# Attention block on one core: the transposes of the attention's output put directly behind the values of their slots, the output products spread differently

## The chip, the cores and the metric

The kernel runs on one core of one Trainium2 chip. The metric is the device time of one execution in microseconds (us), lower is better. A core has a matrix engine, TensorE (PE in the profile, its weight loads PEld), and three elementwise engines, VectorE (DVE), ScalarE (ACT) and GpSimd (POOL). SyncE (SP) issues the DMAs. Every engine runs its own program in order. They wait for each other by semaphores.

## What is computed

The input is 32 batches of 256 tokens by 128 channels. For each batch:

```python
xn  = layernorm(x)
a   = rmsnorm(xn);  q, k, v = a @ Wq, split(a @ Wkv)        # 16 heads of 64
q, k = head_rmsnorm(q), head_rmsnorm(k)
sim = tanh(q @ k.T / 50) * 50 / 8
att = (softmax(sim) @ v) @ Wo
h   = gelu(xn @ (W1 + scale * m1).T + b1)                  # m1, m2 of rank 4, from 16 rows of xn
out = x + att + h @ (W2 + scale * m2).T + b2
```

## The kernel before

The program is one pipeline over batches, fully unrolled. It goes in steps, one for each batch, and a step has eight slots, numbered 0 to 7 here. In slot s of step b the attention works on pair s of heads (two heads) of batch b. Beside that, the same slots hold pieces of other batches: projections of batch b+1 and b+2 (stage 1 and 2 in the tables), and the end of batch b-1 (stage -1): transposing its attention output, and multiplying it by Wo. Which piece stands in which slot of which engine is written out by hand in tables, TENSOR_STEPS, SCALAR_STEPS, VECTOR_STEPS and POOL_STEPS.

The pieces that matter here, with the line of the profile:

- `scores` (L531, TensorE): 12 matmuls for pair s. ScalarE then does `tanh` (L654, `clamped`) and `exp` (L661, `probs`), and GpSimd `lo` (L1073, `probs_lo`).
- `values` (L557 to L559, TensorE): 24 matmuls into the one bank `ps_o`, for the pair two slots back. VectorE then does `divide` (L844, L848, `o_sb`) and, for a pair four slots ahead, `normalise` (L826, `ps_n`), whose factors `rnorm` lie in the same bank as `ps_o`. So `values` of slot s waits for `normalise` of slot s-1: `wait(pe, qk_normed, min(PAIRS * n + s - 1 + NORMALISE_LEAD + 1, PAIRS * batches))`.
- `half` (L669, ScalarE) and `halves` (L835, VectorE): two half-precision parts of a normalised pair.
- `("q", k, a)`, `("k", k, a)`, `("v", k, a)`: projections, three matmuls each (L446 to L448). Piece k of four, called q0, q1 and so on below. ScalarE squares q pieces (L680) and VectorE scales them afterwards (L876); k pieces are copied by ScalarE (L686); v pieces by ScalarE (L691) and VectorE (L881).
- `("oT", k, -1)`: four transposes (L506) of `o_sb` for pairs 2k and 2k+1, copied by ScalarE into `oT` (L694). Called oT0 to oT3.
- `("xT", 0, 2)`, `("low", k, 0)` and `("hid", k, 0)`: transposes of the normed input, the low-rank part of the weights, and the hidden layer (L517), whose gelu is on ScalarE (L699, with an ACT_TABLE_LOAD ahead of it and another one ahead of the next `exp`).
- `("y", n)`: the next n of 24 output products (L567 for the hidden layer, L568 for `oT`) in `ps_y`. Product j of the first token tile needs, from j = 4 on, oT piece (j-4)/2.

All pieces with three entries write one of three banks of `ps_aux`, in turn, in the order of TENSOR_STEPS. Before TensorE writes one, it waits for the reader of the piece three before it (for a q piece that reader is L876 on VectorE, for k and oT pieces it is the copy on ScalarE):

```python
def wait_bank(eng, st, index):
    for back in range(1, 3 * len(AUX)):
        i = index - back * AUX_BANKS
...
        if STAGE[ahead] in (st.stages if rounds == 0 else st.before):
            s, per = AUX_READ[kind]
            wait(eng, s, per * PER_BATCH[kind] * st.batch(ahead + rounds)[0] + per * (k + 1))
            return
```

Of the kernel before, what the change touches and what calls it, by code (L numbers as in the profile page):

```python
# [48 lines left out]

AUX_BANKS = 3  # L50
TENSOR_STEPS = [
# [3 lines left out]
    [("scores",), ("values",), ("hid", 0, 0), ("hid", 1, 0), ("y", 3)],  # L55
# [4 lines left out]
]  # L60
AUX = [(s, *task) for s, tasks in enumerate(TENSOR_STEPS) for task in tasks if len(task) == 3]
assert len(AUX) % AUX_BANKS == 0
# [8 lines left out]


SCALAR_STEPS = [
    [("half", 3), ("q", 3, 1), ("tanh",), ("exp",), ("k", 2, 1), ("k", 3, 1)],
    [("half", 3), ("tanh",), ("oT", 0, -1), ("exp",), ("xT", 0, 2)],
    [("half", 3), ("tanh",), ("oT", 1, -1), ("exp",), ("oT", 2, -1)],
    [("tanh",), ("oT", 3, -1), ("exp",), ("hid", 0, 0), ("hid", 1, 0)],
    [("tanh",), ("q", 0, 2), ("exp",)],
    [("tanh",), ("q", 1, 2), ("exp",), ("v", 0, 1), ("v", 1, 1)],
    [("tanh",), ("exp",), ("k", 0, 2), ("k", 1, 2), ("v", 2, 1)],  # L80
    [("half", 3), ("tanh",), ("v", 3, 1), ("exp",), ("q", 2, 2)],
# [1059 lines left out]
```

How the kernel before makes its waits and increments, by code:

```python
        def wait(eng, s, value):  # L310
            if isinstance(value, int) and value <= 0:
                return
            eng.wait_ge(s, value)
# [38 lines left out]
        def wait_half_hi(eng, b, pair):  # L353
            if pair in GPSIMD_PAIRS:
                eng.wait_ge(half_hi_pool, len(GPSIMD_PAIRS) * b + GPSIMD_PAIRS.index(pair) + 1)
            else:
                eng.wait_ge(half_hi_made, len(SCALAR_PAIRS) * b + SCALAR_PAIRS.index(pair) + 1)
# [10 lines left out]
        @block.sync  # L369
# [19 lines left out]
            def load_rows(st):  # L389
                b, par, _ = st.batch(1)
                normed, used = [v if isinstance(v, int) else sp.to_reg(v) for v in (b + 1, 3 * b)]
                sp.wait_ge(xn_made, normed)
                if isinstance(b, int) and b == 0:
                    sp.wait_ge(rows_cleared, 1)
                wait(sp, sel_copied, used)
                for j in range(2):
                    for at in range(0, ROWS, BLOCK):
                        sp.dma_start(sel_raw[at:at + 2 * RANK, j], xn[1 + j:4 * RANK + j:2, par, 0])\
                            .then_inc(rows_loaded, 16)
# [1 line left out]
            def turn_heads(st, ahead, pair):  # L402
# [5 lines left out]
                        wait_half_hi(sp, b, pair)  # L408
                    else:
                        sp.wait_ge(half_lo_made, PAIRS * b + pair + 1)
                    sp.dma_start(heads_T[:, half, pair].rearrange("p t j n -> p (t j) n"),
# [26 lines left out]
            run_all(sp, run)  # L438
            for par in range(2):
                sp.wait_ge(y_stored[par], 16 * (batches // 2))
```

## Time and profile before

| | before |
|---|---|
| time, median of 3 runs | 1063.51 us (1062.15 to 1065.46) |
| the profiled execution's own time | 1067.33 us |
| its span, first to last instruction | 1065.1 us |
| TensorE busy (matmuls) / weight loads | 97% / 79% |
| VectorE / ScalarE / GpSimd busy | 88% / 92% / 92% |
| granted TensorE clock, mean | 0.994 |

Busy shares are averages over the span. Matmuls are pipelined, so a busy TensorE is not one at its peak; how much it waits is seen from the starts of its matmuls.

### The profile page before, as it was taken

What the parts mean: (1) busy time and instruction counts of PE and PEld (TensorE: products, weight loads), DVE (VectorE), ACT (ScalarE), POOL (GpSimd) and SP (SyncE); (2) the same over time, 40 slices, a digit from 0 to 9 for tenths busy, and PEclk for the clock granted to TensorE, in tenths of its full rate; (3) what the DMA queues carried; (4) which work ended last, traced back from release to release, by engine and by line L of the source; (5) the groups of instructions that cost most, each with busy time, mean ns of one, the idle gap of its engine ahead of it and who ended that gap; (6) DMA issues with size and microseconds to landing.
All of it is one profiled execution on the core that took longest, in us unless ns stands there. A gap on an engine that the chain in (4) does not pass through costs nothing.

```text
span 1065.1 us, 34270 instructions
## 1 busy us (share of the span) xinstructions
PE 1034.3 (97%) x12905; PEld 845.9 (79%) x12905; DVE 937.7 (88%) x2218; ACT 976.0 (92%) x1417; POOL 980.2 (92%) x912
## 2 busy tenths in 40 slices
PE   7689999999999999999999999999999999999997
PEld 6468888788888888888888888888888888888876
DVE  6998999988999988999998999998989998899972
ACT  4599999999999999999999999999999999999995
POOL 6799999999999999999999999999989999999883
PEclk8899999999999999999999999999999999999999
DMA  3354444444445435444444444444454444544351
GB/s 117 56 82 83 81 82 81 73 82 90 77 82 82 77 79 89 77 88 76 79 80 86 78 88 79 76 81 83 81 84 80 72 80 87 82 85 79 71 92 31
DMA packets 310491, 85.44 MB, mean 80 GB/s; under 512 B 282020, under 2 KB 309816, under 8 KB 310328
## 3 DMA queue, kind: packets, MB, share of 16 engines
q1 hardware_dynamic: 310328, 83.25, 43.6%
q8 instruction: 104, 1.70, 0.7%
q14 instruction: 59, 0.48, 0.2%
HBM read 11.09 MB, written 4.19 MB: 14 GB/s over the span
## 4 chain that ended last, share of the span: by engine, by line
PE 44%; POOL 26%; issue 10%; DVE 9%; ACT 5%; SPq 4%; DMA 2%; POOLq 0%; DVEq 0%; ACTq 0%
POOL probs_lo L1073 10%; PE ps_scores L531 9%; PE ps_y L568 5%; PE ps_aux L506 5%; POOL sq_k L1054 5%; POOL halves L1065 4%; PE ps_aux L517 4%; PE ps_o L557 4%; PE ps_aux L446 3%; PE ps_y L567 3%; PE ps_o L559 3%; PE ps_o L558 3%; POOL rstd L984 2%; DVE halves L835 2%; PE ps_aux L447 2%
## 5 line engine op out<-in xcount | busy, mean ns | idle before, releaser
L1073 POOL TENSOR_TENSOR probs_lo<-probs 128x1024 f16<-128x1024 f32 x256 | 485.1, 1895 | 20.6 <-ACT probs L661 19.5
L654 ACT ACTIVATE clamped<-ps_scores 128x1024 f32<-128x1024 f32 x256 | 265.4, 1037 | 43.4 <-PE ps_scores L531 36.3
L661 ACT ACTIVATE probs<-clamped 128x1024 f32<-128x1024 f32 x256 | 272.8, 1066 | 2.6
L557 PEld LDWEIGHTS ps_o<-v_hi,probs 128*128 128x128 bf16 x2048 | 183.7, 98 | 56.6 <-issue 53.5
L531 PE MATMUL ps_scores<-heads_T 64*128 64x256 f16 x3072 | 212.1, 271 | 5.0 <-ACT clamped L654 3.1
L557 PE MATMUL ps_o<-v_hi,probs 128*128 128x65 bf16 x2048 | 214.2, 195 | 2.7 <-DVE ps_n L826 1.1
L558 PE MATMUL ps_o<-v_lo,probs 128*128 128x64 bf16 x2048 | 211.8, 193 | 0.0
L559 PE MATMUL ps_o<-v_hi,probs_lo 128*128 128x65 bf16 x2048 | 211.3, 193 | 0.0
L446 PE MATMUL ps_aux<-w_hi,xhT_hi 128*128 128x512 f32 x384 | 175.3, 456 | 15.0 <-DVE qk L876 10.7
L558 PEld LDWEIGHTS ps_o<-v_lo,probs 128*128 128x128 bf16 x2048 | 187.5, 99 | 0.0
L559 PEld LDWEIGHTS ps_o<-v_hi,probs_lo 128*128 128x128 f16 x2048 | 187.4, 97 | 0.0
L826 DVE TENSOR_TENSOR ps_n<-qk,ps_o 128x512 f32<-128x512 f32 x256 | 175.8, 687 | 0.9 <-issue 0.6
L835 DVE TENSOR_TENSOR halves<-ps_n,halves 128x512 f16<-128x512 f32 x256 | 174.4, 681 | 2.4 <-ACT halves L669 1.4
L531 PEld LDWEIGHTS ps_scores<-heads_T 64*128 64x128 f16 x3072 | 129.3, 94 | 59.0 <-issue 22.8
L1065 POOL TENSOR_TENSOR halves<-qk,rnorm_sb 128x512 f16<-128x512 f32 x128 | 133.2, 1051 | 26.9 <-DVE rnorm_sb L815 14.4
L447 PE MATMUL ps_aux<-w_lo,xhT_hi 128*128 128x512 f32 x384 | 154.0, 401 | 0.0
L448 PE MATMUL ps_aux<-w_hi,xhT_lo 128*128 128x512 f32 x384 | 153.7, 400 | 0.0
L568 PEld LDWEIGHTS ps_y<-wo_sb,oT 128*128 128x128 f32 x1008 | 141.3, 191 | 11.5 <-ACT oT L694 0.9
L568 PE MATMUL ps_y<-wo_sb,oT 128*128 128x128 f32 x1008 | 148.6, 275 | 0.7 <-ACT oT L694 0.7
L1054 POOL TENSOR_TENSOR sq_k<-qk 128x512 f32<-128x512 f32 x128 | 130.7, 1042 | 5.2 <-ACT qk L686 2.9
L848 DVE TENSOR_TENSOR o_sb<-ps_o,rden 128x256 f32<-128x256 f32 x256 | 108.7, 425 | 8.8
L446 PEld LDWEIGHTS ps_aux<-w_hi,xhT_hi 128*128 128x128 f32 x384 | 73.9, 193 | 45.3 <-DVE qk L876 26.8
(96 smaller groups left out, 2009.7 us busy)
## 6 DMA issues: line engine op xcount, KB each, us to landing
heads_T<-halves SPq DMA_TRANSPOSE x512, 2.5
x_in<-in_L_attn_tokens_dram SPq DMA_DIRECT2D x32, 128.0 KB, 2.4
x_res<-in_L_attn_tokens_dram SPq DMA_DIRECT2D x32, 128.0 KB, 2.3
out_dram<-y_sb SPq DMA_DIRECT2D x32, 128.0 KB, 2.0
sel_raw<-xn SPq DMA_DIRECT2D x192, 4.0 KB
qk<-in_L_attn_Wkv_dram SPq DMA_DIRECT2D x2, 512.0 KB, 5.3
qk<-in_L_attn_Wq_dram SPq DMA_DIRECT2D x1, 512.0 KB, 3.5
qk<-in_L_ffn_W_dram SPq DMA_DIRECT2D x2, 256.0 KB
```

Of the source, the lines that this page charges most:

```text
L446: pe.matmul(o, hi_l, hi_r, start=True, stop=False)
L531: ins = pe.matmul(ps_scores[:, odd, t * seq:(t + 1) * seq], heads_T[rows, left, pair, t, k], heads_T[rows, right, pair, :, q], start=(i == ...
L557: pe.matmul(full, hi[:, col], v_hi[:, par, u, h], start=(u == 0), stop=False)
L558: pe.matmul(full[:, 0:DH], hi[:, col], v_lo[:, par, u, h], start=False, stop=False)
L559: ins = pe.matmul(full, probs_lo[:, buf, j, col], v_hi[:, par, u, h], start=False, stop=(u == TT - 1))
L568: return pe.matmul(o, oT[:, pair, tok], wo_sb[:, pair], start=False, stop=(pair == PAIRS - 1))
L654: nc.scalar.activation(clamped[:].rearrange("p j n -> p (j n)"), ps_scores[:].rearrange("p j n -> p (j n)"), ACT.Tanh).then_inc(clamp_done, 1)
L661: nc.scalar.activation(probs[:, pair % RING].rearrange("p j n -> p (j n)"), clamped[:].rearrange("p j n -> p (j n)"), ACT.Exp, bias=LIFT, ...
L835: v.tensor_tensor(halves16[:, pair % 4, 1].rearrange("p a n -> p (a n)"), ps_n[:], halves16[:, pair % 4, 0].rearrange("p a n -> p (a n)"), ...
L1054: g.tensor_tensor(sq_k[:, k % 2], part, part, ALU.mult).then_inc(k_squared, 1)
L1065: g.tensor_tensor(halves16[:, pair % 4, 0].rearrange("p a (h d) -> p a h d", d=DH), pair_of_qk(par, pair).rearrange("p a (h d) -> p a h d" ...
L1073: g.tensor_tensor(probs_lo[:, buf].rearrange("p j n -> p (j n)"), probs[:, buf].rearrange("p j n -> p (j n)"), probs[:, buf].rearrange("p ...
```

## The change

The oT transposes go from places late in slots 0, 1 and 2 (two in slot 2) to the place directly behind `values` in slots 0, 2, 3 and 4. The 24 output products of a step, before 0, 4, 4, 3, 4, 4, 2, 3 over the slots 0 to 7, are now 0, 4, 2, 2, 3, 4, 4, 5. ScalarE's table follows: oT0 ahead of k2 and k3, oT1 behind `exp` of slot 2, oT2 and oT3 between `tanh` and `exp` of slots 3 and 4, and q0 behind `exp` of slot 4 (before: ahead of it). VectorE's, GpSimd's and SyncE's order stay.

```diff
 TENSOR_STEPS = [
-    [("scores",), ("values",), ("k", 2, 1), ("k", 3, 1), ("oT", 0, -1)],
-    [("scores",), ("values",), ("xT", 0, 2), ("low", 0, 0), ("y", 2), ("oT", 1, -1), ("y", 2)],
-    [("scores",), ("values",), ("oT", 2, -1), ("low", 1, 0), ("y", 2), ("oT", 3, -1), ("y", 2)],
-    [("scores",), ("values",), ("hid", 0, 0), ("hid", 1, 0), ("y", 3)],
-    [("scores",), ("values",), ("q", 0, 2), ("q", 1, 2), ("y", 4)],
+    [("scores",), ("values",), ("oT", 0, -1), ("k", 2, 1), ("k", 3, 1)],
+    [("scores",), ("values",), ("xT", 0, 2), ("low", 0, 0), ("y", 4)],
+    [("scores",), ("values",), ("oT", 1, -1), ("low", 1, 0), ("y", 2)],
+    [("scores",), ("values",), ("oT", 2, -1), ("hid", 0, 0), ("hid", 1, 0), ("y", 2)],
+    [("scores",), ("values",), ("oT", 3, -1), ("q", 0, 2), ("q", 1, 2), ("y", 3)],
     [("scores",), ("values",), ("v", 0, 1), ("v", 1, 1), ("y", 4)],
-    [("scores",), ("values",), ("k", 0, 2), ("k", 1, 2), ("y", 2), ("v", 2, 1), ("v", 3, 1)],
-    [("scores",), ("values",), ("q", 2, 2), ("q", 3, 2), ("y", 3)],
+    [("scores",), ("values",), ("k", 0, 2), ("k", 1, 2), ("y", 4), ("v", 2, 1), ("v", 3, 1)],
+    [("scores",), ("values",), ("q", 2, 2), ("q", 3, 2), ("y", 5)],
 ]
 SCALAR_STEPS = [
-    [("half", 3), ("q", 3, 1), ("tanh",), ("exp",), ("k", 2, 1), ("k", 3, 1)],
-    [("half", 3), ("tanh",), ("oT", 0, -1), ("exp",), ("xT", 0, 2)],
-    [("half", 3), ("tanh",), ("oT", 1, -1), ("exp",), ("oT", 2, -1)],
-    [("tanh",), ("oT", 3, -1), ("exp",), ("hid", 0, 0), ("hid", 1, 0)],
-    [("tanh",), ("q", 0, 2), ("exp",)],
+    [("half", 3), ("q", 3, 1), ("tanh",), ("exp",), ("oT", 0, -1), ("k", 2, 1), ("k", 3, 1)],
+    [("half", 3), ("tanh",), ("exp",), ("xT", 0, 2)],
+    [("half", 3), ("tanh",), ("exp",), ("oT", 1, -1)],
+    [("tanh",), ("oT", 2, -1), ("exp",), ("hid", 0, 0), ("hid", 1, 0)],
+    [("tanh",), ("oT", 3, -1), ("exp",), ("q", 0, 2)],
```

On TensorE, in slot 2 of a step in the middle of the program, there stood behind the last matmul of `values` (the names in brackets are the semaphores that a row waits for):

```order
L506 MATMUL ps_aux<-ident,o_sb 128x128 [waits o_normed,xT_split]
L506 MATMUL ps_aux<-ident,o_sb 128x128 x3
L512 MATMUL ps_aux<-low2,sel_rows 128x512 [waits low_made,weff_made]
L568 MATMUL ps_y<-wo_sb,oT 128x128 [waits oT_copied]
L568 MATMUL ps_y<-wo_sb,oT 128x128
L506 MATMUL ps_aux<-ident,o_sb 128x128 [waits o_normed,oT_copied]
L506 MATMUL ps_aux<-ident,o_sb 128x128 x3
L568 MATMUL ps_y<-wo_sb,oT 128x128 [waits oT_copied]
L568 MATMUL ps_y<-wo_sb,oT 128x128
L531 MATMUL ps_scores<-heads_T 128x256 [waits clamp_done,heads_turned3]
L531 MATMUL ps_scores<-heads_T 128x256 x11
L557 MATMUL ps_o<-v_hi,probs 128x65 [waits qk_normed,o_normed,lo_made]
```

At the same place after the change:

```order
L506 MATMUL ps_aux<-ident,o_sb 128x128 [waits o_normed,k_copied]
L506 MATMUL ps_aux<-ident,o_sb 128x128 x3
L512 MATMUL ps_aux<-low2,sel_rows 128x512 [waits low_made,xT_split]
L568 MATMUL ps_y<-wo_sb,oT 128x128 [waits oT_copied]
L568 MATMUL ps_y<-wo_sb,oT 128x128
L531 MATMUL ps_scores<-heads_T 128x256 [waits clamp_done,heads_turned3]
L531 MATMUL ps_scores<-heads_T 128x256 x11
L557 MATMUL ps_o<-v_hi,probs 128x65 [waits qk_normed,o_normed,lo_made]
```

One group of transposes and two products have left the slot, so the scores and values of slot 3 (the last three rows) stand closer behind those of slot 2.

On ScalarE, slots 3 and 4 before the change, from `tanh` of slot 3 on to `tanh` of slot 5:

```order
L654 ACTIVATE clamped<-ps_scores 128x1024 [waits probs_done,scores_done]
L694 COPY oT<-ps_aux 128x512 [waits oT_filled]
L661 ACTIVATE probs<-clamped 128x1024 [waits attended,clamp_done]
L699 ACT_TABLE_LOAD
...
L654 ACTIVATE clamped<-ps_scores 128x1024 [waits probs_done,scores_done]
L680 ACTIVATE sq_q<-ps_aux 128x512 [waits norm2_made,q_filled]
L661 ACT_TABLE_LOAD [waits attended]
L661 ACTIVATE probs<-clamped 128x1024 [waits clamp_done]
L654 ACTIVATE clamped<-ps_scores 128x1024 [waits probs_done,scores_done]
```

And after it:

```order
L654 ACTIVATE clamped<-ps_scores 128x1024 [waits probs_done,scores_done]
L694 COPY oT<-ps_aux 128x512 [waits oT_filled]
L661 ACTIVATE probs<-clamped 128x1024 [waits attended,clamp_done]
L699 ACT_TABLE_LOAD
...
L654 ACTIVATE clamped<-ps_scores 128x1024 [waits probs_done,scores_done]
L694 COPY oT<-ps_aux 128x512 [waits oT_filled]
L661 ACT_TABLE_LOAD [waits attended]
L661 ACTIVATE probs<-clamped 128x1024 [waits clamp_done]
L680 ACTIVATE sq_q<-ps_aux 128x512 [waits norm2_made,q_filled]
L654 ACTIVATE clamped<-ps_scores 128x1024 [waits probs_done,scores_done]
```

The first L694 was oT3 and is now oT2, which TensorE makes in the same slot; the second is oT3; and L680, the square of q0, has moved behind the table load and `exp`.

On TensorE in slot 5, which is alike before and after but for the first wait, the two v projections now read:

```order
L446 MATMUL ps_aux<-w_hi,xhT_hi 128x512 [waits oT_copied]
L447 MATMUL ps_aux<-w_lo,xhT_hi 128x512
L448 MATMUL ps_aux<-w_hi,xhT_lo 128x512
L446 MATMUL ps_aux<-w_hi,xhT_hi 128x512 [waits q_scaled]
L447 MATMUL ps_aux<-w_lo,xhT_hi 128x512
L448 MATMUL ps_aux<-w_hi,xhT_lo 128x512
```

The second (v1) takes the bank of q0 and waits until VectorE has scaled q0, as it did before.

## Rows read from the trace of the kernel before

**Rows 1.** Busy time of each engine, stretches from 100 to 1000 us, summed

```profile
sum 900.00, PE 895.11 PEld 734.54 DVE 817.76 ACT 853.23 POOL 855.86; mean PE 99.46 PEld 81.62 DVE 90.86 ACT 94.80 POOL 95.10
```

**Rows 2.** Waits, 200 to 900 us (22 steps): total us, times, longest

```profile
PEld ps_aux L446 <- DVE qk L876: 12.2, 22, 1.0
```

**Rows 3.** Timeline, TensorE, one step: start us, length us, instruction, count

```profile
518.90 0.83 PE L531 MATMUL ps_scores<-heads_T 64*128 64x256 f16 x12
...
520.94 0.40 PE L448 MATMUL ps_aux<-w_hi,xhT_lo 128*128 128x512 f32 x1
521.41 0.50 PE L446 MATMUL ps_aux<-w_hi,xhT_hi 128*128 128x512 f32 x1
...
522.22 0.60 PE L506 MATMUL ps_aux<-ident,o_sb 128*128 128x128 f32 x4
522.75 0.83 PE L531 MATMUL ps_scores<-heads_T 64*128 64x256 f16 x12
...
528.99 0.60 PE L506 MATMUL ps_aux<-ident,o_sb 128*128 128x128 f32 x4
529.43 0.61 PE L568 MATMUL ps_y<-wo_sb,oT 128*128 128x128 f32 x4
529.97 0.83 PE L531 MATMUL ps_scores<-heads_T 64*128 64x256 f16 x12
...
530.73 0.20 PE L557 MATMUL ps_o<-v_hi,probs 128*128 128x65 bf16 x1
...
531.46 1.97 PE L517 MATMUL ps_aux<-xnT,w_eff 128*128 128x256 f32 x8
...
540.27 0.39 PE L446 MATMUL ps_aux<-w_hi,xhT_hi 128*128 128x512 f32 x1
...
540.96 0.38 PE L567 MATMUL ps_y<-w_eff,hid 128*128 128x128 f32 x2
...
550.68 0.83 PE L531 MATMUL ps_scores<-heads_T 64*128 64x256 f16 x12
```

**Rows 4.** Timeline, ScalarE, the same step

```profile
520.95 1.06 ACT L661 ACTIVATE probs<-clamped 128x1024 f32<-128x1024 f32 x1
521.91 1.09 ACT L686 COPY qk<-ps_aux 128x512 f32<-128x512 f32 x2
523.14 0.59 ACT L669 CAST halves<-ps_n 128x512 f16<-128x512 f32 x1
...
530.87 1.02 ACT L654 ACTIVATE clamped<-ps_scores 128x1024 f32<-128x1024 f32 x1 [0.68 <-PE ps_scores L531]
531.79 0.58 ACT L694 COPY oT<-ps_aux 128x512 f32<-128x512 f32 x1
532.25 1.07 ACT L661 ACTIVATE probs<-clamped 128x1024 f32<-128x1024 f32 x1
533.34 1.28 ACT L699 ACT_TABLE_LOAD   x1
534.63 1.57 ACT L699 ACTIVATE hid<-ps_aux,b_col 128x256 f32<-128x256 f32 x4
536.08 1.04 ACT L654 ACTIVATE clamped<-ps_scores 128x1024 f32<-128x1024 f32 x1
536.99 0.62 ACT L680 ACTIVATE sq_q<-ps_aux 128x512 f32<-128x512 f32 x1
537.62 1.28 ACT L661 ACT_TABLE_LOAD   x1
538.92 1.06 ACT L661 ACTIVATE probs<-clamped 128x1024 f32<-128x1024 f32 x1
```

**Rows 5.** Timeline, VectorE, the same step

```profile
523.94 0.68 DVE L835 TENSOR_TENSOR halves<-ps_n,halves 128x512 f16<-128x512 f32 x1
...
529.00 0.69 DVE L826 TENSOR_TENSOR ps_n<-qk,ps_o 128x512 f32<-128x512 f32 x1
...
538.80 0.66 DVE L876 TENSOR_TENSOR qk<-ps_aux,g_bc 128x512 f32<-128x512 f32 x1
```

## The prediction

> **What bounds the kernel now.** I first read the busy time over the steady part. TensorE's matmuls are busy 99.5% of it, GpSimd 95.1%, ScalarE 94.8%, VectorE 90.9% [rows 1]. With four engines so full, the shares don't say which one sets the pace. The starts in the timeline do. A step takes 31.78 us, from the scores of slot 0 at 518.90 to those of the next step at 550.68 [rows 3]. Inside it I looked for matmuls that start later than their like. There is one regular case: in slot 0, k3's first matmul starts 0.47 us behind the last one of k2 (520.94, 521.41), where such matmuls follow each other at 0.23 us. k3 then takes 0.81 us to the next group, where v1, with its bank free in time, takes 0.69 (540.27 to 540.96) [rows 3]. So this wait costs 0.24 + 0.1 us, about 0.34 in all. The list of waits has it as a weight load of L446 waiting for L876 on VectorE, once in each of 22 steps [rows 2]: k3's bank is that of q2, which VectorE has to scale first. Everything else on TensorE runs without a gap. TensorE is the bound, and it loses some 0.34 us of 31.78.
>
> The Trainium skill (Perfetto Trace Analysis, Identifying the Most-Contended Engine) says that matmul busy time is no measure for TensorE and that the share of weight loads is. That share is 81.6% here, under GpSimd's and ScalarE's. By that page TensorE has room, GpSimd would be the engine to watch, and a new order on TensorE should change little (the third rival below).
>
> **The work itself.** Nothing is added or removed: 16 transposes, 24 products and four copies a step, as before. What goes is a few changes between kinds of work. That is worth under 0.1 us a step in either direction, and I cost it at nothing. So the time comes from waits. I set t = 0 at the scores of slot 0 (518.90) and walk through a step of the new order. Four transposes take 0.44 us (528.99 to 529.43); two products take 0.54 (529.43 to 529.97), of which 0.09 is the change to scores, since four transposes ahead of scores take 0.53 (522.22 to 522.75) [rows 3]. So two products are worth 0.45.
>
> **Slot 0: the old wait goes.** k2 now needs q2's bank and k3 needs q3's. The transposes stand ahead of them, so k2 comes 0.44 later than before, but needs its bank about 0.7 earlier than k3 did. In itself that is 0.26 us worse. But more work (the sum of the last part below, 0.89 us) now lies between the reciprocal roots of slot 4, from which GpSimd's squares and VectorE's sums start, and this point. So I expect this wait to be gone: -0.34.
>
> **Slots 1 to 3: a new wait on VectorE.** Slot 1 loses a group of transposes (-0.44), slot 2 one group and two products (-0.89). The values of slot 3 stood at 530.73, t = 11.83 [rows 3]. TensorE now gets there at 11.83 - 0.34 - 0.44 - 0.89 = 10.16. They must wait for the `normalise` of slot 2. Before, it ran from 529.00 to 529.69, so it ended at t = 10.79 [rows 5], and slack was 1.04. Can VectorE be earlier? From the `halves` of slot 1 (523.94, t = 5.04) to that `normalise` it runs 12 instructions with no idle time [rows 5], and the change leaves their order alone. Their start hangs on ScalarE's `half` of slot 1. ScalarE's `exp` of slot 0 starts at 520.95 and the next instruction 0.96 later; a copy of oT takes 0.46 to the next (531.79 to 532.25), two k copies 0.98; `half` takes 0.59 [rows 4]. So with oT0 ahead of k2 the half ends at 2.05 + 0.96 + 0.46 + 0.98 + 0.59 = 5.04. VectorE's chain starts where it did, and ends at 10.79. TensorE waits from 10.16 to 10.84 (0.05 for the signal, as from a scaling to a matmul), and loses 0.07 to 0.1 on top, as k3 did: **about 0.75 us**. Queued behind it on TensorE are oT2, the hidden layer and all later slots.
>
> **Slots 3 and 4: ScalarE's chain.** Before, oT3 was long made when ScalarE came to it in slot 3. Now oT2 comes from the same slot. The values take 0.73 us (530.73 to 531.46) [rows 3]. The transposes take about 0.63 more until the last one ends, and ScalarE starts 0.07 behind such an end, as `tanh` does (scores end 530.80, `tanh` starts 530.87) [rows 3, 4]. So oT2's copy starts at 10.91 + 0.73 + 0.70 = 12.34. From there ScalarE has no gap [rows 4]: `exp` of slot 3 +0.46, table load +1.09, gelus +1.29, `tanh` of slot 4 +1.45, oT3 +0.91, table load +0.59, `exp` of slot 4 +1.30. That gives 19.43, where before it was 538.92, t = 20.02. And q0, which stood ahead of the table load at 536.99 (t = 18.09), now comes behind `exp`, +0.96: it starts at 20.39 and ends at 21.01.
>
> The table load is in this sum with 1.29 us, from its start to that of the first gelu (533.34 to 534.63) [rows 4]. The Trainium skill (ScalarE: Activation LUTs, What ACT_TABLE_LOAD costs) gives 2.66 us for a switch, a drain of 1.38 included. With that figure both loads would be longer, q0 would come 2.8 us later still, and the step would be some 36 us. The trace shows no such drain and decides.
>
> **Slot 5: v1 waits for q0.** v1 takes q0's bank, so it waits for q0's scaling on VectorE: 0.05 for the signal and 0.66 [rows 5], so at 21.72, and v1 starts at 21.77. Before, the scaling was done at 539.46, and v1 started at 540.27, t = 21.37, with 0.8 to spare [rows 3, 5]. Without waits TensorE would now be there at 21.37 - 0.34 - 0.44 - 0.89 + 0.22 + 0.22 = 20.14 (slots 3 and 4 each gain a group of transposes and lose a product); with the wait of slot 3, at 20.9. So it waits here again, **0.9 us**.
>
> **The step.** Behind v1 TensorE ran for 10.41 us to the next scores (540.27 to 550.68) [rows 3]. Slots 6 and 7 gain two products each, +0.89, and 0.1 is lost to the wait: 11.40. A new step is 21.77 + 11.40 = 33.17 us, 1.39 more than 31.78. It is a closed chain: scores of slot 0, ScalarE to `half` of slot 1, VectorE to `normalise` of slot 2, TensorE's values and oT2, ScalarE to q0, VectorE, v1, and TensorE to the next scores.
>
> The full pattern (q0 of the batch after next, v1 of the next, oT of the last) stands in steps 1 to 29. 29 x 1.39 = 40.3 us. Against the profiled execution's own 1067.33 that is 1107.6; it was 3.8 above the median of the runs, 1063.51, so for the median I get **1104**.
>
> **Rivals.** First, one of the two new waits does not bite, because I have placed VectorE's or ScalarE's chain too late. Without the wait at slot 3, the oT2 copy starts at 10.16 + 0.73 + 0.70 = 11.59, so everything behind it is 0.75 earlier: 32.42 us a step, +0.64 x 29 = +19, 1082. Against it: 12 instructions without idle time [rows 5]. 14%.
>
> Second, faster. If VectorE's `normalise` came by 10.1 and q0 were scaled by 20.1, only the removed wait would be left: -0.34 x 29 = -10, 1054. It turns on whether the last 1.6 us before q0's scaling can vanish; for it speaks only that ScalarE had idle time before (0.68 at one `tanh` [rows 4]), and I have already used that. 5%.
>
> Third, nothing: TensorE's order does not matter since GpSimd paces. GpSimd's 95.1% of 31.78 is 30.2 us of work [rows 1], so it could go on as before, and the time would stay within 0.3% (3.2 us, about what a measurement here can tell from no change). Against it: TensorE has no gaps but the one named. 5%.
>
> Fourth, more waits than I have seen. The scores of slot 3 are now 1.67 us earlier in the step, and the transposed heads that they need come by DMA, issued by SyncE at its own pace; or a wait that was hidden elsewhere comes out. 0.5 us more a step gives 33.7, +55, 1118. 14%.
>
> The forecast itself has 62%; its own range is 1093 to 1111, a third of a microsecond a step either way. The range 1081 to 1116 takes in the first rival and the nearer part of the fourth. Faster 0.05, same 0.05, slower 0.90.
>
> **What would show it.** In the profile after: no wait of L446 for L876 in slot 0, but one in slot 5, with v1's first matmul 0.9 us late. A wait of L557 for VectorE's `ps_n` (L826) once a step, in slot 3, about 0.7 us. ScalarE's q0 behind `exp`, and matmul busy time down from 99.5% to some 95 or 96%, GpSimd's and ScalarE's to about 91%. Slots 1 and 2 shorter, 6 and 7 longer by 0.45 each. I would be wrong if the `halves` of slot 1 started well before t = 5, or if v1's bank were free when TensorE comes.

## The result: 3.7% slower

The changed kernel takes 1103.72 us (median of 4 runs, 1102.64 to 1105.71), the kernel before 1064.49 us in the same comparison. The ratio is 1.0371, with a 95% interval of 1.0341 to 1.040. The profiled execution has a span of 1103.6 us where before it was 1065.1.

Over the same stretches as in [rows 1], the busy time of each engine is now:

```profile
sum 900.00, PE 856.84 PEld 703.13 DVE 780.14 ACT 823.79 POOL 824.24; mean PE 95.20 PEld 78.13 DVE 86.68 ACT 91.53 POOL 91.58
```

All engines have lost three to four points. They do the same work, in a longer step. The list of waits from 200 to 900 us (total us, times, longest) says where TensorE waits:

```profile
PEld ps_aux L446 <- DVE qk L876: 20.3, 21, 1.2
PE ps_aux L446 <- DVE qk L876: 11.1, 21, 0.7
PE ps_o L557 <- DVE ps_n L826: 10.5, 15, 0.7
PEld ps_scores L531 <- DMA heads_T<-halves: 8.3, 6, 1.7
PE ps_scores L531 <- DMA heads_T<-halves: 7.2, 6, 1.5
PE ps_o L557 <- DVE ps_o L803: 4.6, 16, 0.3
```

The first pair of rows is of the kind that stood in [rows 2], but it is another wait now, as the timeline shows. The third is new. The DMA wait is there in six of the 21 steps (the same list of the kernel before has it in one or two of 22). The last row is also new: the values waiting for the Newton steps (L801 to L807). With these, VectorE works out the reciprocal roots for `normalise`, in the bank of `ps_o`. TensorE in one step of the changed kernel, to be read beside [rows 3]:

```profile
540.03 0.83 PE L531 MATMUL ps_scores<-heads_T 64*128 64x256 f16 x12
...
542.46 0.39 PE L448 MATMUL ps_aux<-w_hi,xhT_lo 128*128 128x512 f32 x1
542.69 0.39 PE L446 MATMUL ps_aux<-w_hi,xhT_hi 128*128 128x512 f32 x1
...
549.38 0.83 PE L531 MATMUL ps_scores<-heads_T 64*128 64x256 f16 x12
...
550.91 0.19 PE L557 MATMUL ps_o<-v_hi,probs 128*128 128x65 bf16 x1 [0.70 <-DVE ps_n L826]
...
555.49 0.19 PE L557 MATMUL ps_o<-v_hi,probs 128*128 128x65 bf16 x1 [0.29 <-DVE ps_o L803]
...
560.89 0.40 PE L448 MATMUL ps_aux<-w_hi,xhT_lo 128*128 128x512 f32 x1
561.75 0.50 PE L446 MATMUL ps_aux<-w_hi,xhT_hi 128*128 128x512 f32 x1 [0.47 <-DVE qk L876]
...
573.07 0.83 PE L531 MATMUL ps_scores<-heads_T 64*128 64x256 f16 x12
```

The step takes 573.07 - 540.03 = 33.04 us. k3 in slot 0 follows k2 at 0.23 us (542.46, 542.69): the old wait is gone. In slot 3 the values wait 0.70 us for `normalise`. In slot 4 they wait 0.29 us for the Newton steps. In slot 5 v1 starts 0.86 us behind the matmul ahead of it, where 0.23 is usual: 0.63 us of wait. ScalarE and VectorE in the same step, beside [rows 4, 5]:

```profile
544.37 0.61 ACT L669 CAST halves<-ps_n 128x512 f16<-128x512 f32 x1
...
552.30 0.59 ACT L694 COPY oT<-ps_aux 128x512 f32<-128x512 f32 x1 [0.87 <-PE ps_aux L506]
552.78 1.06 ACT L661 ACTIVATE probs<-clamped 128x1024 f32<-128x1024 f32 x1
...
559.43 1.06 ACT L661 ACTIVATE probs<-clamped 128x1024 f32<-128x1024 f32 x1
560.40 0.58 ACT L680 ACTIVATE sq_q<-ps_aux 128x512 f32<-128x512 f32 x1
```

```profile
545.01 0.69 DVE L835 TENSOR_TENSOR halves<-ps_n,halves 128x512 f16<-128x512 f32 x1 [0.57 <-ACT halves L669]
...
550.08 0.68 DVE L826 TENSOR_TENSOR ps_n<-qk,ps_o 128x512 f32<-128x512 f32 x1
...
561.01 0.69 DVE L876 TENSOR_TENSOR qk<-ps_aux,g_bc 128x512 f32<-128x512 f32 x1 [1.46 <-ACT sq_q L680]
```

One sees the whole chain. ScalarE's half of slot 1 (t = 4.34 from the step's start) releases VectorE, which had idled 0.57 us for it. VectorE reaches `normalise` at t = 10.05. TensorE's values follow, then oT2, for which ScalarE had idled 0.87 us. ScalarE runs on without a gap to q0 (t = 20.37), for which VectorE had idled 1.46 us, and v1 waits for its scaling. Idle time with a releaser stands at each handover, none in between.

### The profile page after: what moved, and what is told of

It is laid out like the page before. It is cut to its first block, busy times and chain, and to the rows that moved or that the text cites. A ratio compares the mean times of both kernels' runs of the same rounds, so it can differ in the third digit from the quotient of the medians.

```text
span 1103.6 us, 34270 instructions
## 1 busy us (share of the span) xinstructions
PE 1030.4 (93%) x12905; PEld 842.3 (76%) x12905; DVE 931.4 (84%) x2218; ACT 981.9 (89%) x1417; POOL 980.9 (89%) x912
## 4 chain that ended last, share of the span: by engine, by line
PE 38%; ACT 27%; DVE 13%; issue 10%; SPq 6%; DMA 4%; POOL 1%; ACTq 0%; DVEq 0%; POOLq 0%
ACT probs L661 8%; PE ps_scores L531 7%; PE ps_aux L446 6%; PE ps_y L568 5%; PE ps_aux L448 4%; PE ps_aux L447 4%; ACT L699 4%; ACT L661 3%; ACT hid L699 3%; DVE halves L835 3%; ACT clamped L654 3%; DMA heads_T<-halves 3%; PE ps_o L557 3%; DVE ps_n L826 3%; PE ps_y L567 3%
## 5 line engine op out<-in xcount | busy, mean ns | idle before, releaser
L568 PE MATMUL ps_y<-wo_sb,oT 128*128 128x128 f32 x1008 | 144.4, 276 | 2.8 <-ACT oT L694 2.8
L876 DVE TENSOR_TENSOR qk<-ps_aux,g_bc 128x512 f32<-128x512 f32 x128 | 85.0, 685 | 47.2 <-ACT sq_q L680 47.2
```

What stands on the lines that cost most here:

```text
L568: return pe.matmul(o, oT[:, pair, tok], wo_sb[:, pair], start=False, stop=(pair == PAIRS - 1))
```

## The experiments

Theory 1 is the chain above: one closed chain through TensorE, ScalarE and VectorE, with another one close behind it, which runs through VectorE's Newton steps. Its rivals were that the waits are independent of each other, or that they are slack which something else would take. Step lengths below are medians over steps 1 to 29, from the starts of slot 0's scores. Places in a step (t) are from the same start, in steps of the usual length.

### q0 ahead of `exp` again

```diff
-    [("tanh",), ("oT", 3, -1), ("exp",), ("q", 0, 2)],
+    [("tanh",), ("oT", 3, -1), ("q", 0, 2), ("exp",)],
```

> The changed kernel with one edit: in slot 4 ScalarE does q0 ahead of exp again (tanh, oT3, q0, exp). Theory 1 (one closed chain, in which v1 waits for q0's scaling): q0 starts at t = 17.95 instead of 20.37, v1's bank is free when TensorE comes, its wait of 0.63 + 0.1 us a step goes, and the wait of slot 3's values for VectorE stays. A step of 33.05 becomes 32.3 us, 21 us less than the changed kernel: about 1083, ratio to the kernel before 1.018. Rival A (v1's wait is only where slack shows, and another wait takes its place, for instance that exp of slot 4, 0.45 us later, delays GpSimd and the values of slot 6): no gain, 1100 to 1104. Rival B (the two new waits are independent and this one is the whole of the loss beyond slot 3's 0.75 us): same as theory 1 in time, told apart by the third kernel of this batch.

Measured: 1083.67 us, ratio to the kernel before 1.019 (1.0172 to 1.0207), and a step of 32.31 us. Its waits from 200 to 900 us:

```profile
PE ps_o L557 <- DVE ps_n L826: 12.2, 18, 0.8
...
PE ps_o L557 <- DVE ps_o L803: 5.1, 18, 0.3
...
PEld ps_aux L446 <- DVE v_lo L881: 0.7, 3, 0.3
```

No wait for L876 is left, the others have about the size that they had, and 0.74 us a step is back. So in the changed kernel q0's place in ScalarE's table costs 20 us of the 39.

### One sum of squares behind slot 2's `normalise`

```diff
-    ... ("normalise",), ("sum", 5, 1), ("sum", 6, 1), ("xT", 0, 2), ("low", 0, 0)],
-    [("halves", 3), ("divide",), ("normalise",), ("sum", 7, 1), ("low", 1, 0)],
+    ... ("normalise",), ("sum", 5, 1), ("xT", 0, 2), ("low", 0, 0)],
+    [("halves", 3), ("divide",), ("normalise",), ("sum", 6, 1), ("sum", 7, 1), ("low", 1, 0)],
```

> The changed kernel with one edit: VectorE sums the squares of one k piece (0.6 us) behind the normalise of slot 2 instead of in slot 1. No work changes, only the normalise of slot 2 comes 0.6 us earlier. Theory 1: slot 3's values start at t = 10.2 instead of 10.8, oT2's copy, the table loads, exp and q0 follow 0.6 earlier, so v1 starts at about 21.1 instead of 21.7, and a step is 32.3 to 32.4 us: 20 us less, about 1084, ratio 1.018. TensorE then waits in slot 4 for the Newton steps instead (about 0.9 us, no work saved, since that chain on VectorE is as long as before). Rival (slot 3's wait for VectorE is slack that v1's wait would swallow anyway, and ScalarE's own queue sets q0): no change, 1100 to 1104.

Measured: 1097.3 us, ratio 1.031 (1.0286 to 1.0334), a step of 32.67 us. The step is 0.38 us shorter, half of what theory 1 said, and more than the rival's nothing. The time gained only 6.4 us of the expected 20. Part of that is in the longer steps: the profiled execution has nine that are over 0.25 us longer than its median, the changed kernel seven. VectorE's timeline in slot 1 shows why the step gained only half:

```profile
542.31 0.68 DVE L778 TENSOR_REDUCE norm<-sq_q 128x8 f32<-128x512 f32 x1
543.11 0.42 DVE L767 TENSOR_TENSOR xhT_lo<-ps_aux,xhT_hi 128x256 fp32r<-128x256 f32 x1
...
545.25 0.69 DVE L826 TENSOR_TENSOR ps_n<-qk,ps_o 128x512 f32<-128x512 f32 x1
```

L767 starts 0.80 us behind the sum, where 0.6 is usual: VectorE now comes to it before ScalarE has copied the transposed input. So slot 2's `normalise` comes only 0.4 us earlier, and the Newton steps 0.2 us later. A step that is 0.38 us shorter fits the 0.4. But this explanation came after the fact, so the next edit repeats the test without that side effect.

### The low-rank weights behind slot 2's `normalise`

```diff
-    ... ("normalise",), ("sum", 5, 1), ("sum", 6, 1), ("xT", 0, 2), ("low", 0, 0)],
-    [("halves", 3), ("divide",), ("normalise",), ("sum", 7, 1), ("low", 1, 0)],
+    ... ("normalise",), ("sum", 5, 1), ("sum", 6, 1), ("xT", 0, 2)],
+    [("halves", 3), ("divide",), ("normalise",), ("low", 0, 0), ("sum", 7, 1), ("low", 1, 0)],
```

> The changed kernel with one edit: VectorE makes the low-rank weights of the hidden layer (L888, 0.66 us) behind the normalise of slot 2 instead of ahead of it. It repeats the test of the moved sum without that one's side effect (there VectorE came 0.2 us too early for ScalarE's copy of the transposed input and waited, so normalise came only 0.4 us earlier, and the Newton steps 0.2 later). Theory 1: normalise 0.66 us earlier, Newton steps where they were in the changed kernel, q0 and v1 0.65 earlier: 32.3 to 32.4 us a step, about 1083, ratio 1.018. Rival (the chain does not run through slot 3's wait; what the moved sum gained had another cause): 32.7 or more, 1095 to 1104.

Measured: 1088.33 us, ratio 1.0219 (1.0203 to 1.0235), a step of 32.40 us. The step is as expected, 0.65 us shorter with no work removed: VectorE's order ahead of slot 2's `normalise` is on the chain. The time is 5 us above the forecast. In the profiled execution six steps are 0.7 to 1.6 us longer than the rest (in the changed kernel six steps, by 0.4 to 0.8); the list of waits has the DMA wait of the scores in four of those between 200 and 900 us, which is taken up below (the edit that removes it was not tried on this kernel). TensorE now waits in slot 4 instead:

```profile
PE ps_o L557 <- DVE ps_o L803: 16.3, 18, 0.9
```

### Both: q0 ahead, and the sum behind `normalise`

The edits are those of the first and second experiment together.

> The changed kernel with both edits above. Theory 1: they are not additive. VectorE's Newton steps end at t = 15.35 as before, the values of slot 4 wait for them, and from there TensorE needs 16.9 us to the next scores: 32.3 us a step again, 1083, ratio 1.018, like each edit alone. Rival B (two independent waits): both go, 31.6 us a step, about 1062, ratio 0.998.

Measured: 1087.14 us, ratio 1.0221 (1.0203 to 1.0238), a step of 32.53 us. Independent waits would have given 31.6 us. Instead the two edits together are no better than q0 alone (32.31), and 0.2 us worse, which is the 0.2 by which the moved sum delays the Newton steps. Its waits:

```profile
PE ps_o L557 <- DVE ps_o L803: 16.1, 20, 0.9
PE ps_o L557 <- DVE ps_n L826: 5.6, 17, 0.4
```

So behind the chain through q0 lies the one through the Newton steps, at 32.3 us a step. The starts show it: the values of slot 4 begin at t = 15.46 with q0 alone ahead and at 15.67 here, and from there TensorE takes the same 16.85 us to the next step in both.

### q0 ahead, and oT0's copy behind ScalarE's half of slot 1

```diff
-    ... ("tanh",), ("exp",), ("oT", 0, -1), ("k", 2, 1), ("k", 3, 1)],
-    [("half", 3), ("tanh",), ("exp",), ("xT", 0, 2)],
+    ... ("tanh",), ("exp",), ("k", 2, 1), ("k", 3, 1)],
+    [("half", 3), ("oT", 0, -1), ("tanh",), ("exp",), ("xT", 0, 2)],
...
-    [("tanh",), ("oT", 3, -1), ("exp",), ("q", 0, 2)],
+    [("tanh",), ("oT", 3, -1), ("q", 0, 2), ("exp",)],
```

> The changed kernel with q0 ahead of exp in slot 4, and ScalarE's copy of oT0 behind the half of slot 1 instead of ahead of k2 and k3 in slot 0. With q0 ahead alone a step took 32.31 us, and theory 1 says that VectorE's Newton steps (end at t = 15.31) and the values of slot 4 behind them bound it, a chain that starts with ScalarE's half of slot 1. The second edit lets that half end 0.3 us earlier (0.46 for the copy, less a wait for k3's matmuls), so a step takes 32.0 us: 9 us less than with q0 ahead alone, 1074 to 1076, ratio 1.010. Rival (VectorE's chain starts with its own work or GpSimd's, not with ScalarE's half): 32.3 us, 1083.

Measured: 1077.72 us, ratio 1.0129 (1.0111 to 1.0147), undisturbed steps of 32.10 to 32.26 us. The direction is right: both of VectorE's chains begin with ScalarE's half of slot 1, and the copy of oT0 that the change puts ahead of it costs here. In the shortest steps the values of slot 4 begin at t = 15.26, 0.2 us earlier than with q0 alone ahead, and again 16.85 us from the next step. The size is 0.1 to 0.3 us a step short of the forecast. A small wait of TensorE came with it, xT (L484) for oT0's copy, whose bank it takes:

```profile
PEld ps_aux L484 <- ACT oT L694: 4.0, 22, 0.2
```

It fits 0.1 us of the shortfall: VectorE's `halves` of slot 1 come 0.31 us earlier than with q0 alone ahead, but its part of the transposed input (L767) only 0.21, since it now starts 0.69 us behind the sum ahead of it (503.25, 503.94), where 0.6 is usual. Whether this wait is all of it was not tried.

### SyncE's row loads behind the transposes of pair 3

```diff
-                    if "front" in st.stages and s == SELECT_SLOT:
-                        load_rows(st)
                     turned = ahead_of(st, s, NORMALISE_LEAD - 1)
                     if turned:
                         turn_heads(st, *turned)
+                    if "front" in st.stages and s == SELECT_SLOT:
+                        load_rows(st)
```

> The changed kernel with one edit: SyncE issues the six small loads of rows (0.67 us each) behind the transposes of pair 3's halves instead of ahead of them. In 8 of the changed kernel's steps the scores of slot 3 waited 0.6 to 1.5 us for those transposes, and these steps took 33.4 to 33.9 us instead of 33.05. If SyncE's queue is what is late, that goes: 4 to 5 us less, 1099, ratio 1.033. If the DMA itself is slow in these steps whatever is issued ahead of it, nothing changes: 1103 to 1104.

Measured: 1100.77 us, ratio 1.0341 (1.0325 to 1.0356). The gain of 3 us is a little under the forecast. But what the edit does to the irregular steps is plain: steps 2 to 29 now all take 33.03 to 33.13 us. The wait of the scores is gone from the list of waits of the whole span, where the changed kernel has it nine times:

```profile
PEld ps_scores L531 <- DMA heads_T<-halves: 12.0, 9, 1.7
PE ps_scores L531 <- DMA heads_T<-halves: 10.2, 9, 1.5
```

What is late is SyncE's queue. In a late step of the changed kernel, SyncE and the scores of slot 3 look like this:

```profile
441.18 4.01 SPq L399 DMA_DIRECT2D sel_raw<-xn  x6
445.29 8.21 SPq L411 DMA_TRANSPOSE heads_T<-halves  x6
```

```profile
450.99 0.83 PE L531 MATMUL ps_scores<-heads_T 64*128 64x256 f16 x12 [1.48 <-DMA heads_T<-halves]
```

Six loads of 4 KB hold the queue for 4 us just ahead of the transposes that slot 3 needs. They do so in every step. In this one the block also starts late, 1.09 us after the step's start instead of 0.12, because one of the two transposes ahead of it took 2.17 us where 1.19 is usual; three more of the late steps have such a slow transpose there. Eight of the 29 steps have the wait, and only the six with 1.1 us and more of it are longer (by 0.4 to 0.8 us): up to about 0.75 us the values would have waited for `normalise` anyway. Why a transpose is sometimes slow stays open.

### The products alone

To the kernel before, only the new numbers of products, with the transposes and ScalarE's table left as they were:

```diff
-    [("scores",), ("values",), ("oT", 2, -1), ("low", 1, 0), ("y", 2), ("oT", 3, -1), ("y", 2)],
-    [("scores",), ("values",), ("hid", 0, 0), ("hid", 1, 0), ("y", 3)],
-    [("scores",), ("values",), ("q", 0, 2), ("q", 1, 2), ("y", 4)],
+    [("scores",), ("values",), ("oT", 2, -1), ("low", 1, 0), ("y", 2), ("oT", 3, -1)],
+    [("scores",), ("values",), ("hid", 0, 0), ("hid", 1, 0), ("y", 2)],
+    [("scores",), ("values",), ("q", 0, 2), ("q", 1, 2), ("y", 3)],
...
-    [("scores",), ("values",), ("k", 0, 2), ("k", 1, 2), ("y", 2), ("v", 2, 1), ("v", 3, 1)],
-    [("scores",), ("values",), ("q", 2, 2), ("q", 3, 2), ("y", 3)],
+    [("scores",), ("values",), ("k", 0, 2), ("k", 1, 2), ("y", 4), ("v", 2, 1), ("v", 3, 1)],
+    [("scores",), ("values",), ("q", 2, 2), ("q", 3, 2), ("y", 5)],
```

> The kernel before with one part of the change: only the output products are spread anew (slots 0 to 7: 0, 4, 2, 2, 3, 4, 4, 5); all transposes and ScalarE's order stay as before. Theory 1: the four products now lie between the values of slot 4 and k3, so k3 finds its bank free (0.34 us a step), slot 3's values come 0.8 us earlier in the step and still find VectorE done (slack 1.04), and v1's q0 is early. TensorE alone would need 31.4 us a step; VectorE's Newton steps, 0.26 us ahead of slot 4's values before, close the next chain at 31.5. So 7 us faster than the kernel before, ratio 0.993 (0.990 to 0.997). Rival (the move of the products itself makes TensorE wait, through the same slots that are now shorter): slower, ratio above 1.003.

Measured: 1061.06 us, ratio 0.9973 (0.996 to 0.9985), a step of 31.55 us in the median, 31.53 in most. The step is as expected, and this half of the change is a gain. The time gained 3 us, less than the 6 to 7 us that the step promises. In the profiled execution 8 of 29 steps are over 0.25 us longer than the median (6 in the kernel before), and the next two experiments price that: the row loads cost more here than in the kernel before. Of k3's wait [rows 2] there remains:

```profile
PEld ps_aux L446 <- DVE qk L876: 1.2, 4, 0.3
```

The Newton steps bound this kernel too. The scores and the first values of slot 4 in the kernel before, and in this one:

```profile
534.03 0.83 PE L531 MATMUL ps_scores<-heads_T 64*128 64x256 f16 x12
534.80 0.21 PE L557 MATMUL ps_o<-v_hi,probs 128*128 128x65 bf16 x1
```

```profile
530.62 0.83 PE L531 MATMUL ps_scores<-heads_T 64*128 64x256 f16 x12
531.58 0.19 PE L557 MATMUL ps_o<-v_hi,probs 128*128 128x65 bf16 x1
```

```profile
531.20 0.23 DVE L803 TENSOR_TENSOR ps_o<-ps_o,newton_r 128x64 f32<-128x64 f32 x1
```

The values start 0.96 us behind the scores instead of 0.77, and 0.15 us behind the end of the Newton step, as in the changed kernel (0.15 behind it, where the wait for L803 is marked). This holds in every step of the usual length.

### The products, and the row loads later

Both edits of the last two experiments, on the kernel before.

> The kernel before with the products spread as in the changed kernel (transposes and ScalarE as before), and SyncE's row loads behind the transposes of pair 3's halves. The products alone gave 31.53 us a step instead of 31.76, but more steps with a wait for the transposed halves (about 6 us over the run, 3 in the kernel before), and so only 0.27% in the time. If the row loads ahead of them are the cause: 4 to 5 us less than with the products alone, 1056, ratio 0.992 to 0.994. If not: 1061, ratio 0.997.

Measured: 1056.82 us, ratio 0.9931 (0.9916 to 0.9946). It beats both kernels. The row loads are worth 0.4% in it (against 0.9973 for the products alone). The products bring slot 3's scores forward, from t = 11.05 to 10.27, so a late transpose has less slack there. That this is why the row loads cost more is argued, not tested by itself.

### The row loads alone

The edit of the row loads on the kernel before, with nothing else.

> The kernel before with one edit: SyncE's row loads behind the transposes of pair 3's halves. It splits the gain of the last kernel (ratio 0.993) between the products and the row loads. The kernel before lost about 3 us over the run in steps longer than 31.76 us; if all of them come from this queue, 1061 to 1062, ratio 0.997, and the products give the other 0.4%. k3's wait of 0.34 us a step stays. If the late transposes cost the kernel before nothing: ratio 1.000, and the row loads matter only together with the products.

Measured: 1062.85 us, ratio 0.9986 (0.9977 to 0.9995), a step of 31.74 us with k3's wait as before. The row loads alone give a little over 0.1%, half of what was expected. The expectation had its 3 us from the profiled execution of the kernel before, which was 3.8 us above the median. The products alone give 0.27%, so some 0.3% of the 0.7% come only with both edits, which is a little more than the intervals allow for chance.

The move of the transposes without that of the products was not run, so its price alone is not known.

## Why the prediction was right, step by step

**What bounds it.** TensorE did set the pace, with a wait of 0.34 us in a step. The prediction said that nothing else had a gap. There was one more, in slot 6, where v3's weights wait for ScalarE's copy of a k piece:

```profile
PEld ps_aux L446 <- ACT qk L686: 5.5, 22, 0.5
```

```profile
546.04 0.19 PEld L446 LDWEIGHTS ps_aux<-w_hi,xhT_hi 128*128 128x128 f32 x1 [0.24 <-ACT qk L686]
```

By the starts of the matmuls this costs 0.07 us a step, and the new spread of the products takes it away too. The products alone bring the step from 31.76 to 31.53, by 0.23 us: 0.34 and 0.07 go, and 0.19 comes back in slot 4, where the values wait for the Newton steps, as the expectation had said. The list of waits of that run has L803 in three steps only; the starts show it in all.

The Trainium skill (Perfetto Trace Analysis, Identifying the Most-Contended Engine) tells to optimise the engine with the highest occupancy first and to judge TensorE by MFU (the share of its peak rate that it uses) and by the share of weight loads. The first was not worked out here. By the weight loads alone (81.6%) that engine was GpSimd. The measurement decides against this reading: with GpSimd's work as it was, taking a wait of 0.34 us from TensorE shortened the step by 0.23 us.

**The work itself at nothing.** The counts of instructions are the same. But TensorE needs less: with the waits taken off, its starts add up to about 31.2 us a step in the changed kernel and 31.35 before (31.76 less 0.34 and 0.07). So this term was mis-sized by some 0.1 us, a little more than the prediction allowed. It changed little, since most of it lies ahead of v1, where the step waits anyway.

**Slot 0.** The wait is gone, as said: k3 follows k2 at 0.23 us.

**Slot 3, the wait for `normalise`.** Forecast: arrival at t = 10.16, first matmul at 10.91, 0.75 us lost. Measured: arrival at 10.11 (549.38, and 0.76 for the scores), first matmul at t = 10.88, 0.77 lost, VectorE's `normalise` from t = 10.05. Moving 0.66 us of VectorE's work behind that `normalise` shortens the step by 0.65. Shown.

**Slots 3 and 4, ScalarE's chain.** oT2's copy was forecast at t = 12.34 and stands at 12.27, q0 at 20.39 and stands at 20.37. From the start of `exp` of slot 3 to that of slot 4 it is 6.65 us, forecast 6.63.

**Slot 5, v1's wait.** Forecast at 21.77, measured 561.75 - 540.03 = 21.72. The wait itself was forecast at 0.9 and is 0.63, since TensorE is not there at 20.9 but at 21.09 (560.89 and 0.23). Behind v1 it runs 11.32 us to the next step, forecast 11.40; v3's wait, which is gone, is most of that difference.

**What the prediction missed** is behind that. The values of slot 4 wait 0.29 us for the Newton steps, which I hadn't named. It cost nothing, because v1's wait lies behind it and is longer. It is no trifle, though: with q0 back in its place it closes the chain at 32.3 us, and the sum of the two other waits alone would have promised 31.6 for both edits together, where 32.53 was measured.

**The step and the sum.** 33.17 was forecast and 33.05 measured; 1.39 more a step forecast, 1.29 measured. 29 x 1.29 = 37.4 us of the 38.5 by which the spans differ. In the profiled executions the steps that are longer than the median add 5.7 us, where they added 4.1 before: 1.6 us more, of which 0.4 lie in step 1. What lies outside the 29 steps is 0.4 us shorter. The other 1.2 us are late transposes, which I had only as a rival (the fourth). The late transposes are there, in the place that it named, and not at the 0.5 us a step of that rival. By the two experiments with the row loads they cost about 3 us of the time in the changed kernel and 1 us in the one before, so 2 us of the difference. That 1104 comes so close to 1103.72 is luck: the term for the steps is 3 us too high, the late transposes were left out (2 us), and the kernel before was 1 us slower in this comparison than the 1063.51 from which the forecast starts. The mechanism was right without luck: both new waits stand where they were forecast, within 0.05 us.

**The rivals.** The first (only one of the two waits bites), the second (faster) and the third (nothing) are refuted by the profile, which has both waits in each undisturbed step. The second rival has a true core: what the change does to the products alone is faster.

## What to carry to other kernels

In a full pipeline, a wait of 0.34 us is no invitation to move work at will: each move shortens some slots, and the slack of the other engines in those slots is what it spends. Follow the chain around the whole period and write down, for each handover, who arrives first and by how much; two waits in one chain don't add up, and behind a removed one stands the next. A list of waits can leave out a small one that comes in every step, and the starts of the matmuls show it. When a change moves several things, price each by itself: here the products were worth a gain, and taking back one entry in ScalarE's order, q0 behind `exp`, brought back half of the loss. And small DMAs in a queue delay what stands behind them by the time of their issue (here 4 us for six), which costs where that is needed soon: 1 to 4 us of the time in the three kernels in which they were moved.

## What the runs showed of the hardware

Each of SyncE's small loads (4 KB) holds its queue for 0.67 us (4.01 us for six, in the changed kernel). For its transposes the trace of the changed kernel, from 200 to 900 us, has:

```profile
L411 SPq DMA_TRANSPOSE heads_T<-halves x337: 1188/1222/2559, 200.0 to 897.5; - x169
...
DMA to landing us min/median/max: 2.4/2.5/4.8
```

So a transpose holds the queue for 1.2 us at the median and up to 2.6, and lands 2.4 to 4.8 us after its issue. I had not expected that spread. With it, the same block of six loads ahead of a transpose costs nothing in most steps, and in others TensorE waits up to 1.5 us.
